# A decoder's cross-attention: key-weighted queries made once in the first stage instead of batch by batch

## What is computed

```python
x = x + rg_lru(_layernorm(x))                       # u, g = two projections; h = g*h + (1-g)*u; out projection
# cross-attention: latents = _layernorm(x), media = ctx_1024
xn = _layernorm(media) * gamma_media + beta_media
ln = _layernorm(latents) * gamma_lat + beta_lat
q = ln @ Wq + bq
kv = concatenate([xn, ln], axis=1) @ Wkv + bkv
k, v = split(kv, 2, axis=-1)                        # then to 8 heads of 128
attn = softmax((q * 128 ** -0.5) @ k.T, axis=-1)
x = x + (attn @ v) @ Wo + bo
# then a mixture of 8 experts, each token to its best one: gelu(x @ W1[e]) @ W2[e], times the gate
```

## Time and profile before

| | us |
|---|---|
| runs | 1229.52, 1224.95, 1229.72 (median 1229.52) |
| the profiled execution | 1225.31 |
| its span in the profile | 1223.6 |
| PE busy | 1126.4 (92%) |
| DVE, ACT, POOL busy | 728.6, 498.3, 353.8 |
| DMA moved | 115 MB, mean 94 GB/s |

### The profile page before, as it was taken

How to read it: one execution, slowest core, us unless ns; L and a number is a source line. 1 busy time by engine, 2 the same in 40 slices (tenths; PEclk the granted TensorE clock), 3 DMA queues, 4 the chain that set the end, 5 groups by cost and what they waited for, 6 DMA issues and landing times.

```text
span 1223.6 us, 19966 instructions
## 1 busy us (share of the span) xinstructions
PE 1126.4 (92%) x6964; PEld 1011.1 (83%) x6965; DVE 728.6 (60%) x1307; ACT 498.3 (41%) x940; POOL 353.8 (29%) x274
## 2 busy tenths in 40 slices
PE   2868988999999999999999999999996699999996
PEld 1857768998998998998998998998984578878775
DVE  6788244745744844664664674574434785774992
ACT  2321353333333343243244234234224484765871
POOL 5483320603603503323233143142100121130222
PEclk9989999999999989999999999999988699999998
DMA  9102572003002002001100200200205695793970
GB/s 299 41 1 96 145 200 85 2 1 86 0 0 84 2 0 64 22 0 47 39 0 14 71 0 6 80 0 0 83 1 177 218 347 200 244 340 104 349 284 28
DMA packets 71935, 114.99 MB, mean 94 GB/s; under 512 B 20045, under 2 KB 20557, under 8 KB 71904
## 3 DMA queue, kind: packets, MB, share of 16 engines
q1 hardware_dynamic: 70144, 109.79, 27.9%
q0 software_dynamic: 1760, 4.79, 1.2%
HBM read 104.71 MB, written 10.84 MB: 94 GB/s over the span
## 4 chain that ended last, share of the span: by engine, by line
PE 64%; DVE 19%; issue 7%; ACT 5%; DMA 4%; POOL 0%; DVEq 0%; SPq 0%; ACTq 0%; POOLq 0%
PE bank L487 14%; PE bank L488 14%; PE bank L489 14%; PE bank L861 5%; PE bank L928 5%; DVE raw L1216 4%; PE bank L921 4%; PE bank L896 3%; DMA stage<-in_W 3%; DVE wsl L1220 2%; PE bank L848 2%; DVE smx L1369 2%; ACT wsh L1151 1%; DVE smx L1364 1%; PE bank L821 1%
## 5 line engine op out<-in xcount | busy, mean ns | idle before, releaser
L487 PE MATMUL bank<-pt_h,xn_h 128*128 128x256 f32 (+1 forms) x576 | 168.2, 292 | 0.7 <-DVE pt_l L1220 0.7
L488 PE MATMUL bank<-pt_l,xn_h 128*128 128x256 f32 (+1 forms) x576 | 165.7, 288 | 0.0
L489 PE MATMUL bank<-pt_h,xn_l 128*128 128x256 f32 (+1 forms) x576 | 165.6, 288 | 0.0
L1220 DVE TENSOR_TENSOR wsl<-stage,wsh 128x2048 fp32r<-128x2048 f32 x64 | 145.5, 2289 | 20.8 <-ACT wsh L1151 18.8
L693 POOL TENSOR_TENSOR xn_l<-raw,xn_h 128x512 fp32r<-128x512 f32 x48 | 66.1, 1409 | 298.9 <-ACT xn_h L1090 298.9
L487 PE MATMUL bank<-xt_h,qt_h 128*128 128x410 f32 (+1 forms) x384 | 137.4, 358 | 1.6 <-DVE qt_l L1220 1.6
L1113 ACT ACTIVATE pr<-bank,smx 128x412 f32<-128x412 f32 x48 | 29.1, 606 | 269.0 <-DVE smx L1369 269.0
L1151 ACT CAST wsh<-stage 128x2048 fp32r<-128x2048 f32 x64 | 122.7, 1918 | 33.8 <-DMA stage<-in_W 21.2
L488 PE MATMUL bank<-xt_l,qt_h 128*128 128x410 f32 (+1 forms) x384 | 134.8, 351 | 0.0
L489 PE MATMUL bank<-xt_h,qt_l 128*128 128x410 f32 (+1 forms) x384 | 134.5, 350 | 0.0
L1363 DVE TENSOR_REDUCE smx<-bank 128x1 f32<-128x412 f32 x48 | 28.1, 585 | 148.1 <-PE bank L489 148.1
(11 more groups left out here) (211 smaller groups left out, 2555.2 us busy)
## 6 DMA issues: line engine op xcount, KB each, us to landing
stage<-in_W SPq DMA_DIRECT2D x64, 1024.0 KB, 7.3
raw<-in_ctx SPq DMA_DIRECT2D x8, 1280.0 KB
scr_q<-qa SPq DMA_DIRECT2D x8, 400.0 KB, 8.2
qb<-scr_q SPq DMA_DIRECT2D x8, 400.0 KB, 11.0
wq<-in_Wq SPq DMA_DIRECT2D x1, 2048.0 KB, 18.9
wk<-in_WkT SPq DMA_DIRECT2D x1, 2048.0 KB, 9.2
wv<-in_Wv SPq DMA_DIRECT2D x1, 2048.0 KB, 7.9
wo<-in_Wo_x SPq DMA_DIRECT2D x1, 2048.0 KB, 14.8
```

Source lines behind the costliest of these rows:

```text
L487: pe.matmul(dest, lh, rh, start=start and k == 0, stop=False)
L488: pe.matmul(dest, lh, rl, start=False, stop=False)
L489: last = pe.matmul(dest, ll, rh, start=False, stop=stop and k == n - 1)
L1220: return dve.tensor_tensor(dst, src, high.bitcast(F32), ALU.subtract)
```

## The change

The eight Q steps of a batch on PE go. In stage 1, after the queries of a half, PE multiplies them with the key weights: for each head and each of four chunks of 128 of the width, one split product of 400 columns (three matmuls). For that wk is loaded once the u and g projections are done, and split by ACT (two copies of 2048 columns, before the latents' high parts) and DVE (two subtractions, before H of the fifth batch); qa is evicted twice by ACT (plain and as high part), and POOL subtracts to get qa_l, behind its eight additions to xin. The 64 results ("units") are evicted with the scale by ACT (even chunks) and DVE (odd ones) into two stage tiles st, which lie over xin, so that both engines first wait until x1 is stored; SP stores each head's tile (128 partitions x 4 batches x 400 floats) to scr_q, which is now 3200 floats a partition and batch. The row constants of a half are one accumulation of 24 matmuls: the key bias is masked to an 8 x 8 diagonal form (bkm), so that all heads come out on 8 partitions. PE walks through: queries of half 0, latents(1), keys of half 0, constants of half 0, then the same for half 1. ACT then waits for all stores of scr_q and scr_c. wv and wo are loaded once all units are done.

In the loop a batch's 1.6 MB of key-weighted queries are loaded as qf a batch ahead. Q is four steps: ACT copies 128x800 to the high part, DVE subtracts three pieces (700, 68 and 32 columns). In the plan they stand at other places: PT5 and PT6 follow each other, then Z(2,0); T4, T5 and T6 follow each other. The context's statistics are split in two halves (B+ 0 after S3, B+ 1 after PT2), and L+ 0 is the norm alone, at the old place of L+ 1. Memory places move accordingly.

```diff
-N_CA, N_WB, N_CC = 9, 2, 12
+N_CA, N_WB, N_CC = 10, 2, 12
-    d_q = dram("scr_q", (B, P, ROWS))
+    d_q = dram("scr_q", (B, P, HEADS * ND * T))
-            ("E", 6), ("N", 6), ("PT", 4), ("V", 1), ("PT", 5), ("Q+", 0), ("Q+", 1), ("PT", 6), ("Q+", 2), ("Q+", 3),
-            ("Z", (2, 0)), ("T+", 0), ("T+", 1), ("Z", (2, 1)), ("T+", 2), ("T+", 3), ("Q+", 4), ("Z", (2, 2)),
-            ("T+", 4), ("T+", 5), ("Q+", 5), ("Q+", 6), ("T+", 6), ("Q+", 7), ("Z", (2, 3)), ("S+", 0), ("X+", 0),
+            ("Z", (1, 3)), ("E", 6), ("N", 6), ("PT", 4), ("V", 1), ("PT", 5), ("PT", 6),
+            ("Z", (2, 0)), ("Q+", 0), ("T+", 0), ("T+", 1), ("Z", (2, 1)), ("Q+", 1), ("T+", 2), ("T+", 3),
+            ("Z", (2, 2)), ("Q+", 2), ("T+", 4), ("T+", 5), ("T+", 6), ("Q+", 3), ("Z", (2, 3)), ("S+", 0), ("X+", 0),
...
+    def free_unit(eng, u):
+        mine = by_act[u]
+        eng.wait_ge(s_qe if mine else s_qd, sum(x == mine for x in by_act[:u + 1]))
...
-            sp.wait_ge(s_op, B)
+            sp.wait_ge(s_ugp, 4 * ND)
             sp.dma_start(wk[:], a["WkT"].rearrange("(h p) d -> p h d", p=P)).then_inc(s_wk, 16)
...
+                for h in range(HEADS):
+                    acts, dves = stage_rows(half, h)
+                    sp.wait_ge(s_qe, acts)
+                    sp.wait_ge(s_qd, dves)
+                    sp.dma_start(d_q[half * HALF:(half + 1) * HALF, :, h * ND * T:(h + 1) * ND * T].rearrange(
+                        "b p n -> p b n"), st[h % 2][:].rearrange("p b c t -> p b (c t)")).then_inc(s_qout[h % 2], 16)
...
+            pool.wait_ge(s_x1r, B)
+            low_queries(0)
+            low_queries(1)
...
                 for h in range(HEADS):
+                    pe.wait_ge(s_wkl, h // 4 + 1)
+                    pe.wait_ge(s_qal, half * HEADS + h + 1)
+                    for dc in range(ND):
+                        free_unit(pe, u - 4)
+                        part = (slice(None), h, slice(dc * P, (dc + 1) * P))
+                        split_products(pe, bank[u % 4][:, 0:HT], [((wk_h[part], wk_l[part]), (qa_h[:, h, :], qa_l[:, h, :]))],
+                                       True, True).then_inc(s_qp, 1)
+                        u += 1
+                split_products(pe, zbank[half][0:HEADS, 0:HT],
+                               [((bkm_h[:, h, :], bkm_l[:, h, :]), (qa_h[:, h, :], qa_l[:, h, :])) for h in range(HEADS)],
+                               True, True).then_inc(s_cp, 1)
...
-                        for hh in range(4):
-                            h = hg * 4 + hh
-                            last = pe.matmul(qbank[k % 4][:, hh * T:(hh + 1) * T], wk[:, h, dc * P:(dc + 1) * P],
-                                             qb[:, h * T:(h + 1) * T], start=True, stop=True)
-                        last.then_inc(s_qp2, 1)
...
+                elif by_act[u]:
                     n = half * HEADS + h
+                    if n >= 2:
+                        act.wait_ge(s_qout[h % 2], 16 * (n // 2))
+                    act.wait_ge(s_qp, u + 1)
+                    act.activation(st[h % 2][:, :, dc, :], bank[u % 4][:, 0:HT].rearrange("p (b t) -> p b t", b=HALF),
+                                   ACT.Identity, scale=float(DH) ** -0.5).then_inc(s_qe, 1)
...
+            act.wait_ge(s_cout, 16 * 2)
+            for s in s_qout:
+                act.wait_ge(s, 16 * HEADS)
...
+                        act.copy(qt_h[:, k, 0:ROWS].rearrange("p (h t) -> p h t", h=HEADS), qf[:, :, k, :]
+                                 ).then_inc(s_hi, 1)
...
+                        low(qt_l[:, k, 0:m].rearrange("p (h t) -> p h t", t=T), qf[:, 0:HEADS - 1, k, :],
+                            qt_h[:, k, 0:m].rearrange("p (h t) -> p h t", t=T)).then_inc(s_qread, 1)
+                        low(qt_l[:, k, m:m + n], qf[:, HEADS - 1, k, 0:n], qt_h[:, k, m:m + n]).then_inc(s_qread, 1)
+                        low(qt_h[:, k, ROWS:ROWS + RLAST], qf[:, HEADS - 1, k, n:T], qt_h[:, k, m + n:ROWS]
+                            ).then_inc(s_qread, 1)
```

More of the change, by code:

```diff
@@ L279, in build @@
     mem.at = base
-    stage = [mem(f"stage{k}", [P, 4, FC]) for k in range(4)]
+    late = [mem(f"stage{k}", [P, 4, FC]) for k in (2, 3)]
     xg_h = mem("xg_h", [P, ND, TILE], F32R)
@@ L285, in build @@
     ohp = mem("ohp", [P, B, P])
+    stage = [mem(f"stage{k}", [P, 4, FC]) for k in (0, 1)] + late
+    assert mem.at == base_b
     wsh, wsl = [], []
@@ L434, in build, with stage_rows @@
     stds = [e for e in norms if e[0] in "AB"]
+    q_units = []
+    for half in range(2):
+        q_units += [("q", half, h, 0) for h in range(HEADS)]
+        q_units += [("k", half, h, dc) for h in range(HEADS) for dc in range(ND)]
+    by_act = [what == "q" or dc % 2 == 0 for what, _, _, dc in q_units]
+    def free_unit(eng, u):
+        mine = by_act[u]
+        eng.wait_ge(s_qe if mine else s_qd, sum(x == mine for x in by_act[:u + 1]))
+    def stage_rows(half, h):
+        last = half * (HEADS + HEADS * ND) + HEADS + h * ND + ND - 1
+        return sum(by_act[:last + 1]), last + 1 - sum(by_act[:last + 1])
     slot_plan = [("M", 0), ("W", 0), ("M", 1), ("H", 0), ("W", 1), ("M", 2), ("H", 1), ("W", 2), ("O", 0), ("W", 3),
@@ L548, in _ @@
                 sp.dma_start(d_ln[b], xh[0:T, b, :]).then_inc(s_lnout, 16)
+            for b in range(B):
+                sp.wait_ge(s_x1r, b + 1)
+                sp.dma_start(d_x1[b], xin[0:T, b, :]).then_inc(s_out_a, 16)
             sp.wait_ge(s_lnout, 16 * B)
@@ L1046, in _ @@
                     high_weight(3 + e)
-            act.wait_ge(s_bqs, 1)
             act.wait_ge(s_hsl, ND)
+            for k in range(2):
+                act.wait_ge(s_wk, 16)
+                act.copy(wk_h[:, 4 * k:4 * k + 4, :], wk[:, 4 * k:4 * k + 4, :]).then_inc(s_wkh, 1)
             def latents(half):
@@ L1305, in _ @@
                 elif what == "H":
-                    low_rows(g, B + g, tbank[g % 2], s_tel)
-            dve.wait_ge(s_qe, 2 * HEADS)
+                    if g == HALF:
+                        for k in range(2):
+                            dve.wait_ge(s_wkh, k + 1)
+                            part = (slice(None), slice(4 * k, 4 * k + 4), slice(None))
+                            low(wk_l[part], wk[part], wk_h[part]).then_inc(s_wkl, 1)
+                    low_rows(g, B + g, tbank[g % 2], s_tel)
+            dve.wait_ge(s_out_a, 16 * B)
+            for u, (what, half, h, dc) in enumerate(q_units):
+                if not by_act[u]:
+                    n = half * HEADS + h
+                    if n >= 2:
+                        dve.wait_ge(s_qout[h % 2], 16 * (n // 2))
+                    dve.wait_ge(s_qp, u + 1)
+                    dve.tensor_scalar(st[h % 2][:, :, dc, :], bank[u % 4][:, 0:HT].rearrange("p (b t) -> p b t", b=HALF),
+                                      float(DH) ** -0.5, None, ALU.mult).then_inc(s_qd, 1)
+            dve.wait_ge(s_qp, len(q_units))
             ch.add(dve.memset(x2b[:], 0.0))
```

216 lines of the change are left out of this document (111 added, 105 removed), and 4 rows, old and new, of the table plan.

## The result

The kernel after takes **1285.2 us** (median of 4 runs, 1285.1 to 1285.3) against 1228.8 of before on the same chip: ratio **1.047, interval 1.044 to 1.049**. That is 17 us above the forecast of 1268 and inside its range of 1247 to 1293, on the side that was forecast. The profiled executions have spans of 1283.4 and 1223.6, 59.8 apart; what follows divides these 59.8.

What follows compares the result with a forecast made beforehand. PE, busy 92% of the span, was taken as the bound. From the profiled 1225.3 us, 32.2 + 9.4 + 1.7 + 6 + 1.9 - 9 = +42.2 gave 1267.5, stated as 1268, range 1247 to 1293.

Steps and rivals of the forecast that it cites:

- Net PE work: Stage 1: 240 new matmuls at 0.183 us, 44.0, less 11.8 for removed row constants: +32.2 us, nothing hiding it.
- Later start: Stage 1: key products wait for qa_l behind POOL's additions, so PE starts at 142 instead of 132.56: +9.4 us.
- Half clock at the start: Stage 1: the first key products run at half clock after PE's wait: +1.7 us.
- Stores: Stage 1: two stage tiles make a head take 2.8 us instead of 2.2: +6 us for both halves, bounds 0 and 36.
- Into the first batch: From the row constants' end to the first S step: +1.9 us, bounds -0.5 and +5.
- The loop: Removed Q steps had covered hand-overs: -2.7 us a pass, net -1.3 after slow clock, -9 in seven passes.
- slow clock costs 1.6 today; I take 3.0: Loop: half clock after PE idling costs 1.6 us a pass before the change, taken as 3.0 after it.
- The slots after the loop: Behind the loop: the slots were expected to stay unchanged.
- Rival 1: Loop: Q steps hide nothing, all 8.8 us a pass go, 1215 us; decided by PE waiting under 3 at PT6 and T6; 6%.
- Rival 2: Whole kernel: no visible change, loop at its best (-30) and stage 1 at its least (39), 1234 us; 7%.
- Rival 3: Stage 1: stores land at the old median of 9.5 us, 30 more, 1297 us; 7%.
- Rival 4: Stage 1 keys: PE waits for every store and stays at half clock, 17 to 19 us more, 1286; 14%.

Runs made afterwards that it cites:

- four tiles: The kernel after with four stage tiles instead of two, two over xin and two over xh: 1281.5 us, ratio 1.041.
- the filler version: The kernel after with 23 extra unused 100-column matmuls per loop pass in PE's waits around PT5, PT6 and T6: 1256.2 us, ratio 1.020.
- the 16 increments: The kernel after with 16 increments of an unawaited semaphore on GpSimd ahead of the first batch: 1282.8 us, ratio 1.044.
- the order: The kernel after with Q0 before Z(2,0), and Q1 and Q2 before Z(2,1) and Z(2,2) but behind T0/T1 and T2/T3: 1266.7 us, ratio 1.030.
- the version with the early start: The kernel after with GpSimd's query low parts before its additions, stage tiles over xh, x1 stores behind half 0's stores: 1273.3 us, ratio 1.035.

## Why the prediction came out as it did

Right in sign, mechanism and range; 17 too low. By its own steps:

- **Net PE work, +32.2.** Right. A half without store waits takes 17.5 for 96 products, and the constants 4.36 each: 43.7 less the old 11.8 is 31.9.
- **Later start, +9.4 (142).** It was +12.3 (144.8), 2.9 off. 1.1 of it stands already where nothing differs (DVE ends its norms 1.1 later), and is no more than the spread between executions: the first transposes of the latents begin between 100.8 and 106.8 in versions of after with the same code up to there, and between 103.7 and 106.4 in those of before. The prediction took a middle between 139.3 and 145.5; the sum by the Trainium skill ("SBUF — State Buffer", section "SBUF: two separate sides"), 143.9, becomes 145.0 with the 1.1 by which everything began later. Here the trace agrees with the rule: POOL lost 4.1 of the 4.5 us that DVE's subtractions took, and DVE nothing. Putting the low parts first gave 6.0 back.
- **Half clock at the start, +1.7.** Right: twelve products at about 0.33 instead of 0.18 each.
- **Stores, +6.** They cost 4.0 in this execution, shown by four tiles (up to 6.9 in others). Landing was 3.7 with 0.37 to issue, 4.1 instead of 4.4 in all. The two terms 0.7 for the issue and 0.9 for the receipt were not right one by one: the issue is 0.37, and no run shows the receipt by itself. The figure of the Trainium skill ("DMA: Bandwidth & Descriptors", section "Anatomy of one DMA — SWDGE (gpsimd) path") for another queue had given 3.9 for a store, nearer than my sum from old rows; the trace agrees with it within 0.2.
- **Into the first batch, +1.9.** It was +2.9: 17.8 from the constants' end to the first S step.
- Together stage 1 was forecast at +51.2 and gave +52.8.
- **The loop, -1.3 a pass.** Without half clock the working holds to the tenth: 93.3 - 2.7 = 90.6, and the filler version runs at 90.6. **The step that failed is the size of one term: "slow clock costs 1.6 today; I take 3.0".** It was 4.3 on average. The new waits were in place: T6's is 2.2 (forecast 2.4); from PT5 to Z(2,0) 2.8 is waited in three pieces, of which the 1.3 at PT5 is an old one, so 1.5 is new (forecast 2.2). What was wrong is how long half clock lasts around them: 10 us from PT5 on and 3.5 behind T6 in five of six passes. The trace of before had the case to price this from, though not among the rows: the pass of 98.0 us, with 10 us at half clock, is 4.7 over the full-clock pass. A pass changed by 0.0 instead of -1.3, 8 in six, and the stretch from the first S step to the first addition, counted as the seventh, by +3.9 instead of -1.3; the last gave 1.1 back. That is 12 of the 17.
- **The slots after the loop, unchanged.** They were 4.1 longer, of which 2.8 are one instruction fetch of GpSimd. That was left out altogether: code added to an engine moves where its instruction fetches fall, as the 16 increments showed. The Trainium skill ("Runtime: NRT & Kernel Launch", section "Instruction fetch mechanics") states that fetches run ahead of the code in blocks and are mostly hidden; here one was not: the gap was 5.09 instead of 0.96, and cost 2.8.
- **Rivals.** Rival 1 (Q steps hide nothing) is refuted by the version with three quarters of them left out: 5.4 removed a pass, 2.7 gained. By its own sign it was near: PE waits 3.1 a pass at PT6 and T6, and 3 was its limit. Rival 2 needed the loop at its best, which only the fillers and the order reach, and stage 1 at 39. Rival 3 falls with landings of 3.7. Rival 4 named 1286, close to the result, for a wrong reason: the key products came back to full clock after twelve, and the lost time was in the loop.

It was in part luck that the number came out 17 off and not more: behind the same waits a pass of before took 93.3, 94.9 or 98.0, and one of after 92.4 or 95.4.

Open: why the same waits are followed by half clock of different length, or by none, in passes of the same kernel (92.4 and 95.4 in after and in the version with the early start, without an edit there).

## What to carry to other kernels

Before taking work off the busiest engine, ask which hand-overs it covered: here 7.2 us of PE steps were worth 2.7. Then price the clock behind each short wait from the longest such stretch that any pass shows, not from a mean over passes (here the pass of 98.0), and try a few matmuls into an unused bank in that wait: 6 a pass made the old kernel 1.1% faster and 23 a pass gave 29 us to the new one. Put them only where the wait is certain and shorter fillers than the wait; ahead of work that others wait for they cost more than they give. And when a stage that nobody edited changes length, look for an instruction fetch in the gap, and split the stage at the instruction that waits for it: what lies behind may differ by chance. Before a shift is put down to an edit, look at a point ahead of the edit in both traces.

## What was not expected of the hardware

- One PE wait of 1.3 or 1.4 us was enough for half clock right behind it. How long it lasts is not set by the wait: the same wait of before was followed by none (2 passes), 3 to 3.5 us (3) and 10 us (1); with waits of 0.9 and 0.7 behind it, after had 10 us (5) and 6.5 (1). A wait of 2.2 was followed by 3.5 us five times and by none once, and by none four times in six in the version with the early start. With fillers in the waits the granted clock stayed at 1.00 over 544 us.
- GpSimd and DVE beside each other on SBUF operands: GpSimd took 14.0 instead of 9.9 for eight additions, DVE's two subtractions of 2.2 each were not slowed; the row of before had DVE as the loser (7.7 instead of 2.3). Who loses can go either way.
- One instruction fetch of GpSimd made a gap of 5.09 us instead of 0.96 and cost 2.8 us, and 16 idle instructions elsewhere took it away.
